# Even-step probabilities turned by VectorE and DMA instead of TensorE, and one outer loop written out

## The chip, the cores and the metric

The kernel runs on one core of a Trainium2 chip. The metric is the device time of one execution in microseconds (us); lower is better. A core has TensorE (matrix products and 128x128 transposes, written to PSUM), VectorE, ScalarE and GpSimd (elementwise work; in the profile DVE, ACT and POOL), SyncE (SP, which here only issues DMAs), an on-chip memory SBUF of 128 partitions, and the eight banks of PSUM. The engines run their own queues and wait for each other by semaphores.

## The reference

The input is `x` (32 x 64 tokens of width 512) with a context of the same shape. The reference computes

- `h = layernorm(x)`, `q = h Wq` in 32 heads of 128, `k = ctx Wk` and `v = ctx Wv` in 8 heads of 128 (each shared by 4 query heads);
- root-mean-square normalisation of `q` and `k` over the 128 elements of a head, with weights;
- `probs = softmax(q k / sqrt(128) + mask)` over the 64 keys of the same batch entry, `attn = probs v`, and `x = x + tanh(g_x) * attn Wo`;
- then a second layernorm and a feed-forward part: a shared SiLU network and 16 experts, of which each token takes its best two, added with `tanh(g_f)`.

Everything is float32. The change touches only the attention.

## The kernel before, in words

**Stages.** First the keys and values of all tokens are computed (to about 205 us), then come the attention steps (to about 1070 us), then the feed-forward part.

**Attention steps.** There are `STEPS` = 64 steps, i = 0 to 63: 8 groups of query heads (one for each key head) times 8 chunks of 256 tokens. The program counts them as i = 2 d + odd. In step i TensorE computes the queries of step i + 1 (`q_head`, twice, L610 to L612, each product as three products of a high and a low part), the product of step i - 1's probabilities with the values (`probs_v`, L738), the scores of step i + 1 (`scores`, L691), in even steps the transposes of step i's probabilities (`transpose_probs`, L723; in odd steps these stand between the two halves of the second `q_head`), and the output projection of step i - 1 (`outputs`, with `project_out` and `add_quarters`, L705, between its parts).

VectorE computes in step i: the sums of squares of the new queries (`turn_squares` L1526, a transpose of 32x32 blocks; `sum_squares` L1532; `split_sums` L1540 and L1542, whose result `sqs_hl` feeds `add_quarters`), the low part of the attention output (`a_rest`, L1517), the low part of the turned probabilities (`probs_lo`, L1596 in even and L1593 in odd steps), the sums of the squares per head (L1555, L1560), the addition of a projected tile to `acc` (`add_out`, L1511), and the softmax of step i + 1 (L1567 to L1587, result `pb`), at the end a slice of the next group's weights (`slice_lo`, L1601). GpSimd takes the inverse root between (L501) and splits the values (L507, L509). ScalarE copies and squares the queries (L1148, L1156), copies the attention output (L1183) and the turned probabilities (`probs_hi`, L1175 even, L1172 odd), splits weights (`split_slice`, L1187) and takes the exponentials (`exps`, L1161).

**Keys and probabilities as they lie.** The keys are turned by 32x32 blocks on VectorE (`turn_keys`), stored to the DRAM tensor `kbuf`, and loaded by `load_k` (L337) with the blocks in their turned places. The probabilities are turned by TensorE into PSUM: bank 6 in even steps, banks 2 and 3 in odd ones. Bank 6 also receives `project_out(0, ...)`.

**Loads.** SyncE's queue runs `next_loads(d, odd)`: in odd steps four `kt` loads; then a slice of weights (`wraw`, L379), once the slice before has been split (`w_hi`, `w_lo`); then the values `vt` (L385), once the values before have been split (`v_split`).

**Loops.** On each engine steps 0 to 7 stand first, then a hardware loop `Fori(0, 3)` over `gg`, whose body is two groups of 8 steps (steps 8 to 23, 24 to 39, 40 to 55), then the last group. Within a group an inner hardware loop runs over pairs of steps. All order is by hand: the queues are the program text, and the waits are on counts.

Of the kernel before, what the change touches and what calls it, by code (L numbers as in the profile page):

```python
# [32 lines left out]
F32 = mybir.dt.float32  # L33
# [8 lines left out]
P = 128  # L42
# [7 lines left out]
NC = T // CT  # L50
CB = CT // S
STEPS = KVH * NC
TURNED = (3, STEPS - NC)
E, EI = 16, 128
# [12 lines left out]
def build(nc, x, ctxT, wk, wv, w_att, w_shd, mask, g_x, g_f, q_w, k_w, gate, w_gu, w_dn, out):  # L67
    kbuf = nc.dram_tensor("kbuf", [KVH, NC // 2, 4, P, P], F32, kind="Internal").ap()
    vbuf = nc.dram_tensor("vbuf", [STEPS, P, CT], F32, kind="Internal").ap()
    h2buf = nc.dram_tensor("h2buf", [T, D], F32, kind="Internal").ap()  # L70
    ybuf = nc.dram_tensor("ybuf", [2 * T + 2 * P, D], F32, kind="Internal").ap()

    k_ld = kbuf.rearrange("g r l (q j) (c i) -> (g r) c j (l q) i", q=4, c=4)
    k_st = kbuf.rearrange("g r l p n -> r l p g n")
    v_st = vbuf.rearrange("(g c) p (b t) -> c b p g t", g=KVH, b=2)
# [3 lines left out]
    with ExitStack() as ctx:  # L79
# [144 lines left out]
        oh1 = sb("oh1", [P, NT, E])  # L224
        oh2 = sb("oh2", [P, NT, E])
        sgt = [sb(f"sgt{q}", [P, D]) for q in range(1)]
        aft = [sb(f"aft{q}", [P, D]) for q in range(1)]
# [57 lines left out]

        mark = sem("mark")
        ctx_first = [sem("ctx_first0"), sem("ctx_first1")]

        block = ctx.enter_context(nc.Block())

        def turned(j):
# [19 lines left out]
        def _(sp):  # L311

            for s in (v_stored, k_stored, *h2_stored, wgu_last):
                sp.sem_inc(s, 16)
# [55 lines left out]

            def next_loads(d, odd, x_tiles=()):

                i = 2 * d + odd
                if odd:
                    sp.wait_ge(s_done, i + 1)
                    load_k(d + 1)
                sp.wait_ge(w_hi, i + 8)
                sp.wait_ge(w_lo, i + 8)
                sp.dma_start(wraw[:], w_att[i + NC]).then_inc(wr_in, 16)  # L379
                for n in x_tiles:  # L380
                    if n >= 2:
                        sp.wait_ge(x1_done, n - 1)
                    sp.dma_start(xt3[n % 2][:], x[n]).then_inc(x3_in[n % 2], 16)
                sp.wait_ge(v_split, 2 * i + 2)
                sp.dma_start(vt[:].rearrange("p b t -> p (b t)"), vbuf[i + 1]).then_inc(vt_in, 16)  # L385

            with sp.Fori(0, (STEPS - NC) // 2) as d:
                for odd in range(2):
                    next_loads(d, odd)

            for t in range(NC - 1):
# [223 lines left out]
        def _(pe):  # L615
# [141 lines left out]

            def outputs(r, w_before, w_o, o_ready=None, turn=True):
                pe.wait_ge(acc_done, 2 * r + 1)
                project_out(1, w_before, (0, 1))  # L760
                if turn:
                    add_quarters(r + 2)
                project_out(1, w_before, (2, 3))
                if o_ready is not None:
                    pe.wait_ge(w_lo, o_ready)
                pe.wait_ge(pT_evac, 2 * r + 4)
                pe.wait_ge(a_hi, 4 * r + 6)
                pe.wait_ge(a_lo, 4 * r + 6)
                pe.wait_ge(acc_done, 2 * r + 2)
                project_out(0, w_o, (0, 1, 2, 3))  # L770

            def step(d, odd, pair_q, w_q, w_before, w_o, q_ready=None, o_ready=None, last=False, turn=True):


                i = 2 * d + odd
                if q_ready is not None:
                    pe.wait_ge(w_lo, q_ready)
                pe.wait_ge(q_sq, 2 * i + 1)
                q_head(0, 1 - odd, pair_q, w_q).then_inc(q_done, 1)
                pe.wait_ge(q_sq, 2 * i + 2)  # L780
                q_head(1, 1 - odd, pair_q, w_q, (0, 1))
                if last:
                    pe.wait_ge(ss_turned, i + 1)
                    transpose_h2(0, 2)
                    pe.wait_ge(s_scaled, i + 1)
                    transpose_h2(1, 3)
                if odd:
                    transpose_probs(i, odd)
                q_head(1, 1 - odd, pair_q, w_q, (2, 3)).then_inc(q_done, 1)
                probs_v(i - 1, 1 - odd)  # L790
                if last:
                    pe.wait_ge(h2T_lo, 2)
                scores(d + odd, 1 - odd)
                if not turn:
                    q_sums(i + 1)
                if last:
                    transpose_h2(2, 0)
                    transpose_h2(3, 1)
                if not odd:
                    pe.wait_ge(acc_done, 2 * i)  # L800
                    transpose_probs(i, odd)
                outputs(i - 1, w_before, w_o, o_ready, turn)

# [58 lines left out]
            group(0, 0, first=True)  # L862
            with pe.Fori(0, KVH // 2 - 1) as gg:
                for p in range(2):
# [214 lines left out]
        def _(act):  # L1079
# [87 lines left out]

            def probs_hi(i, odd, bank=2):
                act.wait_ge(pT_done, i + 1)
                if odd:  # L1170
# [19 lines left out]
            def act_step(d, odd, w, sl):  # L1190
# [4 lines left out]
                if odd:  # L1195
                    probs_hi(i, 1)
                q_out(1, i + 1)
                squares(1, i + 1)
                a_hi_tile(i - 1, 0)
                if not odd:  # L1200
                    probs_hi(i, 0)
                a_hi_tile(i - 1, 1)
                split_slice(i, w, sl)
                exps(i + 1)

# [35 lines left out]
            act_group(0, 0, 2)  # L1241
            with act.Fori(0, KVH // 2 - 1) as gg:
                for p in range(2):
# [140 lines left out]
        def _(dve):  # L1384
# [158 lines left out]

            def softmax(j, *meanwhile):
                per_row = lambda t: t[:].unsqueeze(2).to_broadcast([P, 8, S])
# [17 lines left out]
                if meanwhile:  # L1563
                    meanwhile[0]()
                dve.wait_ge(q_rt, j + 1)
                dve.wait_ge(s_done, j + 1)
                dve.tensor_tensor(pb[:], PS[3][:].rearrange("p (b s) -> p b s", s=S), per_row(qr),  # L1567
                                  ALU.mult).then_inc(s_scaled, 1)
# [20 lines left out]
            def probs_lo(i, odd, bank=2):  # L1589
# [4 lines left out]
                else:  # L1594
                    dve.wait_ge(pT_hi, 2 * i + 2)
                    dve.tensor_tensor(pt_even(1), pT_even(), pt_even(0), ALU.subtract).then_inc(pT_evac, 2)  # L1596

# [15 lines left out]
            def dve_step(d, odd, w, sl, tile_before, tile, complete=(None, None), turn=True):  # L1613

                i = 2 * d + odd
                if turn:
                    turn_squares(i + 1, 0)
# [12 lines left out]
                if complete[1] is not None:  # L1630
                    residual(complete[1], 0)
                if turn and not odd:
                    probs_lo(i, 0)
# [9 lines left out]

                softmax(i + 1, while_root, while_exp)
                if odd or not turn:
# [32 lines left out]
            dve.memset(g_hl[:].rearrange("p k e -> p (k e)").bitcast(F32), 0.0).then_inc(const_dve, 1)  # L1678
            with dve.Fori(0, KVH // 2 - 1) as gg:
                for p in range(2):  # L1680
# [349 lines left out]
```

## Time and profile before

| | us |
|---|---|
| median of 3 runs | 1386.31 (1386.3 to 1386.43) |
| the profiled execution, its own time | 1385.93 |
| its span | 1384.2 |
| TensorE busy | 1370.0 (99% of the span) |
| VectorE busy | 1020.1 (74%) |
| ScalarE busy | 506.7 (37%) |
| GpSimd busy | 359.3 (26%) |
| mean DMA rate over the span | 90 GB/s |

The span is the stretch from the first to the last recorded instruction of the profiled execution; its own time is what the device took with what lies around the span. Busy time of TensorE counts pipelined matmuls whose ends are modelled, so distances between the starts of neighbouring instructions say more than durations. TensorE's granted clock is 1.0 of full speed throughout.

### The profile page before, as it was taken

The page shows a single profiled execution, that of the slowest core. Times are in us where ns is not written, and L with a number is a line of the kernel's source. Part 1 is how long each engine was busy: PE and PEld are TensorE (multiplying, and loading weights), DVE is VectorE, ACT ScalarE, POOL GpSimd, SP SyncE. Part 2 cuts the span into 40 slices and gives each one's busy share as a digit, 9 for nine tenths or more (in the row PEclk, how much of TensorE's full clock was granted, in tenths as well). Part 3 has the DMA queues.
Part 4 walks back from the last instruction along what each step waited for, and adds up shares of the span by engine and source line. Part 5 has one row for each costly group of instructions (what it writes and reads, how often), then busy time and mean ns, then how long its engine had stood idle before and what let it go on. Part 6 is the DMA issues. An engine that isn't in the chain of part 4 may idle for free.

```text
span 1384.2 us, 26710 instructions
## 1 busy us (share of the span) xinstructions
PE 1370.0 (99%) x8629; PEld 1107.8 (80%) x8630; DVE 1020.1 (74%) x2151; ACT 506.7 (37%) x1085; POOL 359.3 (26%) x374
## 2 busy tenths in 40 slices
PE   9999999999999999999999999999999999999998
PEld 7888877888888887888887888888787888777777
DVE  7555558888888888888888888888688745244459
ACT  5323244343434343434343434434334421222242
POOL 1222232212121212121212121221212100467646
PEclk9999999999999999999999999999999999999999
DMA  6644431111111111111111111111223244554548
GB/s 223 206 135 148 132 94 39 44 38 44 31 43 39 42 38 37 39 42 39 35 44 39 40 33 46 36 42 31 65 62 100 99 160 188 174 193 167 167 147 309
DMA packets 150119, 125.54 MB, mean 91 GB/s; under 512 B 74256, under 2 KB 116240, under 8 KB 149776
## 3 DMA queue, kind: packets, MB, share of 16 engines
q1 hardware_dynamic: 142512, 99.71, 24.2%
q0 software_dynamic: 7520, 24.65, 5.3%
q8 instruction: 58, 0.95, 0.3%
q14 instruction: 29, 0.24, 0.1%
HBM read 86.84 MB, written 37.49 MB: 90 GB/s over the span
## 4 chain that ended last, share of the span: by engine, by line
PE 79%; DVE 4%; issue 1%; DMA 1%; ACT 0%; DVEq 0%; POOL 0%; ACTq 0%
PE ps L610 19%; PE ps L612 18%; PE ps L611 18%; PE ps L999 6%; PE ps L691 5%; PE ps L738 4%; PE ps L1015 3%; PE ps L723 2%; PE ps L994 1%; DVE acc L1960 1%; DVE acc L1967 1%; PE ps L912 1%; PE ps L746 0%; PE ps L1046 0%; PE ps L699 0%
## 5 line engine op out<-in xcount | busy, mean ns | idle before, releaser
L507 POOL CAST vth<-vt 128x256 fp32r<-128x256 f32 x64 | 25.4, 397 | 535.9 <-PE ps L738 533.9
L610 PE MATMUL ps<-hT,w0h 128*128 128x512 f32 (+1 forms) x384 | 152.2, 396 | 1.2 <-DVE w0l L1435 1.2
L1183 ACT CAST ah<-ps 128x256 fp32r<-128x256 f32 x256 | 83.0, 380 | 187.1 <-PE ps L612 180.7
L612 PE MATMUL ps<-hT,w0h 128*128 128x512 f32 (+1 forms) x384 | 149.9, 390 | 0.0
L611 PE MATMUL ps<-hT,w0l 128*128 128x512 f32 (+1 forms) x384 | 149.6, 390 | 0.0
L501 POOL TENSOR_TENSOR qr<-qv,mhalf 128x8 f32<-128x8 f32 x64 | 105.1, 1642 | 157.7 <-DVE qv L1560 131.0
L1148 ACT ACTIVATE qs<-ps,wqk 128x512 f32<-128x512 f32 x128 | 88.2, 689 | 119.3 <-PE ps L612 119.3
L1511 DVE TENSOR_TENSOR acc<-ps,acc 128x512 f32 (+1 forms) x128 | 88.0, 687 | 52.9 <-PE ps L612 52.5
L1161 ACT ACTIVATE pb<-pb 128x256 f32<-128x256 f32 x128 | 48.3, 418 | 167.2 <-DVE pb L1578 167.2
L610 PE MATMUL ps<-w0l,ah 128*128 128x512 f32 x256 | 105.7, 413 | 0.0
L610 PE MATMUL ps<-w1l,ah 128*128 128x512 f32 x256 | 105.0, 410 | 0.0
L1517 DVE TENSOR_TENSOR al<-ps,ah 128x256 fp32r<-128x256 f32 x256 | 96.0, 417 | 11.3 <-ACT ah L1183 10.3
L1526 DVE STREAM_TRANSPOSE sqT<-sq 128x512 f32<-128x512 f32 x108 | 76.6, 709 | 35.6 <-ACT sq L1156 31.4
L610 PE MATMUL ps<-hT,w1h 128*128 128x512 f32 (+1 forms) x256 | 101.3, 396 | 0.0
L612 PE MATMUL ps<-w0h,ah 128*128 128x512 f32 x256 | 100.2, 391 | 0.0
L612 PE MATMUL ps<-w1h,ah 128*128 128x512 f32 x256 | 100.1, 391 | 0.0
L611 PE MATMUL ps<-w0h,al 128*128 128x512 f32 x256 | 100.0, 391 | 0.0
L612 PE MATMUL ps<-hT,w1h 128*128 128x512 f32 (+1 forms) x256 | 100.0, 391 | 0.0
L611 PE MATMUL ps<-w1h,al 128*128 128x512 f32 x256 | 100.0, 391 | 0.0
L611 PE MATMUL ps<-hT,w1l 128*128 128x512 f32 (+1 forms) x256 | 99.7, 390 | 0.0
L999 PE MATMUL ps<-wgu,xgT 128*128 x376 | 94.9, 382 | 0.4 <-issue 0.4
L610 PEld LDWEIGHTS ps<-hT,w0h 128*128 128x128 f32 x384 | 72.1, 188 | 16.5 <-DVE w0l L1435 1.4
(248 smaller groups left out, 3183.7 us busy)
## 6 DMA issues: line engine op xcount, KB each, us to landing
wraw<-in_w_att SPq DMA_DIRECT2D x64, 256.0 KB, 2.6
vbuf<-vo SPq DMA_DIRECT2D x16, 512.0 KB, 3.3
kbuf<-ko SPq DMA_DIRECT2D x16, 512.0 KB, 5.1
kt<-kbuf SPq DMA_DIRECT2D x128, 64.0 KB, 2.2
vt<-vbuf SPq DMA_DIRECT2D x64, 128.0 KB, 2.1
wgu<-in_w_gu SPq DMA_DIRECT2D x4, 2048.0 KB, 8.5
y<-ybuf SPq DMA_DIRECT2D x16, 512.0 KB, 5.9
xt<-in_x SPq DMA_DIRECT2D x16, 256.0 KB, 5.3
```

The lines of the kernel that those rows point to most:

```text
L501: pool.tensor_tensor(qr[:], qv[:], mhalf[:, 0:8], ALU.pow).then_inc(q_rt, 1)
L610: pe.matmul(dst, l_hi, r_lo, start=first, stop=False)
L611: pe.matmul(dst, l_lo, r_hi, start=False, stop=False)
L612: return pe.matmul(dst, l_hi, r_hi, start=False, stop=last)
L691: mm = pe.matmul(PS[3][h * S:(h + 1) * S, b * S:(b + 1) * S], qs[:, h, b], kt[:, b, :], start=True, stop=True)
L738: mm = pe.matmul(PS[4 + b2][:, bp * 256:(bp + 1) * 256], vhl[v_part][rows, bp, :], pt[p_part][rows, 2 * part + bp, :], start=(z == 0), sto ...
L999: mm = pe.matmul(PS[2 + q][:, 0:2 * EI], xgT[q][:, k, :], wgu[:, bass.ds(e, 1), k * 2 * EI:(k + 1) * 2 * EI].rearrange("p a n -> p (a n)") ...
L1148: act.activation(qs[:, h].rearrange("p b s -> p (b s)"), PS[h][:], ACT.Copy, scale=wqk[:, 0:1]).then_inc(q_copy, 1)
L1183: act.copy(ah[:, bp, :, b2, :], pv_view(bp, b2)).then_inc(a_hi, 1)
L1511: dve.tensor_tensor(dst, PS[6 + bp][:], dst, ALU.add).then_inc(acc_done, 1)
L1517: dve.tensor_tensor(al[:, bp, :, b2, :], pv_view(bp, b2), ah[:, bp, :, b2, :], ALU.subtract).then_inc(a_lo, 1)
L1526: dve.transpose(sqT[:].rearrange("p n i -> p (n i)"), sq[:, h].rearrange("p b s -> p (b s)")).then_inc(sq_turned, 1)
```

## The change

In the even steps from 4 to 54 (`by_dma`, 26 steps) the probabilities `pb` are no longer turned by TensorE. VectorE turns them by 32x32 blocks into `pbT`, SyncE stores `pbT` to a DRAM tensor `pbuf` (256 KB), waits for the store to land, and loads the blocks back with four DMAs (64 KB each) into `pt_raw`, so that the whole is the 128x128 transposes' result. ScalarE's high copy and VectorE's low part read `pt_raw` instead of PSUM; `probs_hi` moves from between the two `a_hi_tile` to behind `split_slice` and ahead of `exps`, and `probs_lo` from behind `a_rest` to behind the softmax. On SyncE the store stands ahead of the `wraw` load of the even step, the wait for it and the four loads ahead of the `vt` load. TensorE no longer waits in those steps for bank 6 to be read before `project_out(0, ...)`. The odd steps, steps 0 and 2, and those of the last group are turned as before.

The loop over `gg` becomes a Python loop on TensorE, ScalarE and VectorE: its body stands three times in their programs. The inner loops stay, and so does GpSimd's; SyncE's loop over pairs is as before but begins at step 4.

```diff
--- before.py
+++ after.py
@@ -50,6 +50,7 @@
 NC = T // CT
 CB = CT // S
 STEPS = KVH * NC
+BY_DMA = (4, STEPS - NC)
 TURNED = (3, STEPS - NC)
 E, EI = 16, 128
 SI = 512
@@ -66,11 +67,13 @@
 
 def build(nc, x, ctxT, wk, wv, w_att, w_shd, mask, g_x, g_f, q_w, k_w, gate, w_gu, w_dn, out):
     kbuf = nc.dram_tensor("kbuf", [KVH, NC // 2, 4, P, P], F32, kind="Internal").ap()
+    pbuf = nc.dram_tensor("pbuf", [P, 4, P], F32, kind="Internal").ap()
     vbuf = nc.dram_tensor("vbuf", [STEPS, P, CT], F32, kind="Internal").ap()
     h2buf = nc.dram_tensor("h2buf", [T, D], F32, kind="Internal").ap()
     ybuf = nc.dram_tensor("ybuf", [2 * T + 2 * P, D], F32, kind="Internal").ap()
 
     k_ld = kbuf.rearrange("g r l (q j) (c i) -> (g r) c j (l q) i", q=4, c=4)
+    p_ld = pbuf.rearrange("(q j) c n -> c j q n", q=4)
     k_st = kbuf.rearrange("g r l p n -> r l p g n")
     v_st = vbuf.rearrange("(g c) p (b t) -> c b p g t", g=KVH, b=2)
     h2_t = h2buf.rearrange("(n p) d -> n p d", p=P)
@@ -223,6 +226,9 @@
         rb = sb("rb", [P, NT, E])
         oh1 = sb("oh1", [P, NT, E])
         oh2 = sb("oh2", [P, NT, E])
+        with ExitStack() as a:
+            pbT = sb("pbT", [P, 4, 4, 32], F32, a)
+            pt_raw = sb("pt_raw", [P, 4, 4, 32], F32, a)
         sgt = [sb(f"sgt{q}", [P, D]) for q in range(1)]
         aft = [sb(f"aft{q}", [P, D]) for q in range(1)]
         rab = sb("rab", [P, NT, E], BF16)
@@ -284,9 +290,22 @@
 
 
         mark = sem("mark")
+        p_turned, p_out, p_back = sem("p_turned"), sem("p_out"), sem("p_back")
         ctx_first = [sem("ctx_first0"), sem("ctx_first1")]
 
         block = ctx.enter_context(nc.Block())
+
+        def by_dma(i, odd):
+
+            return not odd and (not isinstance(i, int) or BY_DMA[0] <= i < BY_DMA[1])
+
+        def pT_before(i, d):
+
+            if not isinstance(i, int):
+                return d + 2
+            if BY_DMA[0] <= i < BY_DMA[1]:
+                return i // 2 + 2
+            return i if i < BY_DMA[0] else i - (BY_DMA[1] - BY_DMA[0]) // 2
 
         def turned(j):
 
@@ -310,7 +329,7 @@
         @block.sync
         def _(sp):
 
-            for s in (v_stored, k_stored, *h2_stored, wgu_last):
+            for s in (v_stored, k_stored, p_out, *h2_stored, wgu_last):
                 sp.sem_inc(s, 16)
 
             def first_context(tt):
@@ -368,12 +387,21 @@
             sp.wait_ge(hT_lo, NT)
             sp.dma_start(graw[:], gate).then_inc(g_in, 16)
 
-            def next_loads(d, odd, x_tiles=()):
+            def next_loads(d, odd, x_tiles=(), k=None):
 
                 i = 2 * d + odd
+                if k is not None:
+                    sp.wait_ge(p_turned, k + 1)
+                    sp.wait_ge(p_back, 64 * k + 64)
+                    sp.dma_start(pbuf, pbT[:].rearrange("p c m i -> p c (m i)")).then_inc(p_out, 16)
                 if odd:
                     sp.wait_ge(s_done, i + 1)
                     load_k(d + 1)
+                if False:
+                    if k is not None:
+                        probs_back(k)
+                    sp.wait_ge(v_split, 2 * i + 2)
+                    sp.dma_start(vt[:].rearrange("p b t -> p (b t)"), vbuf[i + 1]).then_inc(vt_in, 16)
                 sp.wait_ge(w_hi, i + 8)
                 sp.wait_ge(w_lo, i + 8)
                 sp.dma_start(wraw[:], w_att[i + NC]).then_inc(wr_in, 16)
@@ -381,12 +409,27 @@
                     if n >= 2:
                         sp.wait_ge(x1_done, n - 1)
                     sp.dma_start(xt3[n % 2][:], x[n]).then_inc(x3_in[n % 2], 16)
-                sp.wait_ge(v_split, 2 * i + 2)
-                sp.dma_start(vt[:].rearrange("p b t -> p (b t)"), vbuf[i + 1]).then_inc(vt_in, 16)
-
-            with sp.Fori(0, (STEPS - NC) // 2) as d:
+                if not False:
+                    if k is not None:
+                        probs_back(k)
+                    sp.wait_ge(v_split, 2 * i + 2)
+                    sp.dma_start(vt[:].rearrange("p b t -> p (b t)"), vbuf[i + 1]).then_inc(vt_in, 16)
+
+            def probs_back(k):
+                sp.wait_ge(p_out, 16 * k + 32)
+                sp.wait_ge(pT_evac, 4 * k + 6)
+                for c in range(4):
+                    sp.dma_start(pt_raw[32 * c:32 * c + 32].rearrange("p q m i -> p q (m i)"),
+                                 p_ld[c]).then_inc(p_back, 16)
+
+            sp.sem_inc(p_back, 64)
+            for d in range(BY_DMA[0] // 2):
                 for odd in range(2):
                     next_loads(d, odd)
+            with sp.Fori(0, (BY_DMA[1] - BY_DMA[0]) // 2) as k:
+                next_loads(k + BY_DMA[0] // 2, 0, k=k)
+                next_loads(k + BY_DMA[0] // 2, 1)
+            sp.wait_ge(pT_evac, 2 * BY_DMA[1] - 2)
 
             for t in range(NC - 1):
                 next_loads((STEPS - NC) // 2 + t // 2, t % 2, {0: (), 1: (0, 1), 2: ()}.get(t, (2 * t - 4, 2 * t - 3)))
@@ -755,7 +798,7 @@
                 if ks[-1] == KD - 1:
                     mm.then_inc(gu_done, 1)
 
-            def outputs(r, w_before, w_o, o_ready=None, turn=True):
+            def outputs(r, w_before, w_o, o_ready=None, turn=True, bank_free=False):
                 pe.wait_ge(acc_done, 2 * r + 1)
                 project_out(1, w_before, (0, 1))
                 if turn:
@@ -763,7 +806,8 @@
                 project_out(1, w_before, (2, 3))
                 if o_ready is not None:
                     pe.wait_ge(w_lo, o_ready)
-                pe.wait_ge(pT_evac, 2 * r + 4)
+                if not bank_free:
+                    pe.wait_ge(pT_evac, 2 * r + 4)
                 pe.wait_ge(a_hi, 4 * r + 6)
                 pe.wait_ge(a_lo, 4 * r + 6)
                 pe.wait_ge(acc_done, 2 * r + 2)
@@ -796,10 +840,11 @@
                 if last:
                     transpose_h2(2, 0)
                     transpose_h2(3, 1)
-                if not odd:
+                dma = turn and by_dma(i, odd)
+                if not odd and not dma:
                     pe.wait_ge(acc_done, 2 * i)
                     transpose_probs(i, odd)
-                outputs(i - 1, w_before, w_o, o_ready, turn)
+                outputs(i - 1, w_before, w_o, o_ready, turn, dma)
 
             for k in range(KD):
                 pe.wait_ge(w_lo, k + 1)
@@ -860,7 +905,7 @@
                     step(d0 + NC // 2 - 1, 1, 0, W[1 - p], W[p], W[p], q_ready=i0 + 12)
 
             group(0, 0, first=True)
-            with pe.Fori(0, KVH // 2 - 1) as gg:
+            for gg in range(KVH // 2 - 1):
                 for p in range(2):
                     group(NC // 2 + NC * gg + NC // 2 * p, 1 - p)
             group((STEPS - NC) // 2, 1, last=True)
@@ -1165,8 +1210,13 @@
                 q_out(h, 0)
                 squares(h, 0)
 
-            def probs_hi(i, odd, bank=2):
-                act.wait_ge(pT_done, i + 1)
+            def probs_hi(i, odd, bank=2, d=None):
+                if by_dma(i, odd):
+                    act.wait_ge(p_back, 64 * d)
+                    act.wait_ge(pv_done, 2 * i + 2)
+                    act.copy(pt_even(0).rearrange("p m (q i) -> p q m i", q=4), pt_raw[:]).then_inc(pT_hi, 2)
+                    return
+                act.wait_ge(pT_done, pT_before(i, d) + 1)
                 if odd:
                     for q in range(2):
                         act.copy(pt_odd(0, q), pT_odd(q, bank)).then_inc(pT_hi, 1)
@@ -1193,14 +1243,18 @@
                 q_out(0, i + 1)
                 squares(0, i + 1)
                 if odd:
-                    probs_hi(i, 1)
+                    probs_hi(i, 1, d=d)
                 q_out(1, i + 1)
                 squares(1, i + 1)
                 a_hi_tile(i - 1, 0)
-                if not odd:
+                if not odd and not by_dma(i, odd):
                     probs_hi(i, 0)
                 a_hi_tile(i - 1, 1)
+                if by_dma(i, odd) and False:
+                    probs_hi(i, 0, d=d)
                 split_slice(i, w, sl)
+                if by_dma(i, odd):
+                    probs_hi(i, 0, d=d)
                 exps(i + 1)
 
             def act_group(d0, p, t0=0):
@@ -1239,7 +1293,7 @@
             exps(3)
             act_step(1, 1, W[1], 3)
             act_group(0, 0, 2)
-            with act.Fori(0, KVH // 2 - 1) as gg:
+            for gg in range(KVH // 2 - 1):
                 for p in range(2):
                     act_group(NC // 2 + NC * gg + NC // 2 * p, 1 - p)
 
@@ -1541,7 +1595,7 @@
                 dve.wait_ge(sq_sums, k + 3)
                 dve.tensor_tensor(sqs_hl[:, 1, :], flat, sqs_hl[:, 0, :], ALU.subtract).then_inc(sq_part, 1)
 
-            def softmax(j, *meanwhile):
+            def softmax(j, *meanwhile, turn_before=None):
                 per_row = lambda t: t[:].unsqueeze(2).to_broadcast([P, 8, S])
                 dve.wait_ge(ss_done, j + 2)
 
@@ -1564,6 +1618,8 @@
                     meanwhile[0]()
                 dve.wait_ge(q_rt, j + 1)
                 dve.wait_ge(s_done, j + 1)
+                if turn_before is not None:
+                    dve.wait_ge(p_turned, turn_before)
                 dve.tensor_tensor(pb[:], PS[3][:].rearrange("p (b s) -> p b s", s=S), per_row(qr),
                                   ALU.mult).then_inc(s_scaled, 1)
                 if len(meanwhile) > 2:
@@ -1593,6 +1649,11 @@
                         dve.tensor_tensor(pt_odd(1, q), pT_odd(q, bank), pt_odd(0, q), ALU.subtract).then_inc(pT_evac, 1)
                 else:
                     dve.wait_ge(pT_hi, 2 * i + 2)
+                    if by_dma(i, odd):
+                        dve.tensor_tensor(pt_even(1).rearrange("p m (q i) -> p q m i", q=4), pt_raw[:],
+                                          pt_even(0).rearrange("p m (q i) -> p q m i", q=4),
+                                          ALU.subtract).then_inc(pT_evac, 2)
+                        return
                     dve.tensor_tensor(pt_even(1), pT_even(), pt_even(0), ALU.subtract).then_inc(pT_evac, 2)
 
             def slice_lo(i, w, sl):
@@ -1613,6 +1674,11 @@
             def dve_step(d, odd, w, sl, tile_before, tile, complete=(None, None), turn=True):
 
                 i = 2 * d + odd
+                if by_dma(i, odd):
+                    dve.wait_ge(p_ready, 2 * i + 2)
+                    dve.wait_ge(p_out, 16 * (d - 1))
+                    dve.transpose(pbT[:].rearrange("p c m i -> p (c m i)"),
+                                  pb[:].rearrange("p (m z) (h j) -> p (z h) m j", z=2, h=2)).then_inc(p_turned, 1)
                 if turn:
                     turn_squares(i + 1, 0)
                 if odd:
@@ -1629,7 +1695,7 @@
                 a_rest(i - 1, 0)
                 if complete[1] is not None:
                     residual(complete[1], 0)
-                if turn and not odd:
+                if turn and not odd and not by_dma(i, odd):
                     probs_lo(i, 0)
 
                 def while_root():
@@ -1641,7 +1707,9 @@
                 def while_exp():
                     add_out(2 * i, 0, tile)
 
-                softmax(i + 1, while_root, while_exp)
+                softmax(i + 1, while_root, while_exp, turn_before=d - 1 if by_dma(i, odd) else None)
+                if by_dma(i, odd):
+                    probs_lo(i, 0)
                 if odd or not turn:
                     slice_lo(i, w, sl)
 
@@ -1676,7 +1744,7 @@
             dve.wait_ge(pool_const, 6)
             dve.tensor_copy(trib[:], tri[:]).then_inc(const_dve, 1)
             dve.memset(g_hl[:].rearrange("p k e -> p (k e)").bitcast(F32), 0.0).then_inc(const_dve, 1)
-            with dve.Fori(0, KVH // 2 - 1) as gg:
+            for gg in range(KVH // 2 - 1):
                 for p in range(2):
                     group(NC // 2 + NC * gg + NC // 2 * p, 1 - p)
             dve.wait_ge(g_hi_ok, 1)
```

## Rows read from the trace of the kernel before

**Rows 1.** The page: busy us, share of the span and instructions of each engine.
```profile
PE 1370.0 (99%) x8629; PEld 1107.8 (80%) x8630; DVE 1020.1 (74%) x2151; ACT 506.7 (37%) x1085; POOL 359.3 (26%) x374
```

**Rows 2.** Attention: us, busy PE, PEld, DVE, ACT, POOL, clock, DMA share, GB/s.
```profile
240.00:1070.00 830.00, 828.11 (x5890) 675.24 (x5889) 699.33 (x1521) 329.63 (x759) 167.40 (x181) 1.00 0.17 44
```

**Rows 3.** Waits of TensorE: us in total, times, the longest.
```profile
PE ps L705 <- DVE sqs_hl L1542: 1.4, 2, 0.9
```

**Rows 4.** Timeline, TensorE, an odd step: start us, us, engine, instruction.
```profile
600.18 1.15 PE L691 MATMUL ps<-kt,qs 128*64 128x64 f32 x32
...
601.27 0.50 PE L610 MATMUL ps<-w1l,ah 128*128 128x512 f32 x1
```

**Rows 5.** Timeline, TensorE, the even step behind it.
```profile
613.46 1.15 PE L691 MATMUL ps<-kt,qs 128*64 128x64 f32 x32
...
614.96 0.47 PE L610 MATMUL ps<-w1l,ah 128*128 128x512 f32 x1
...
616.19 0.19 PEld L705 LDWEIGHTS ps<-sqs_hl,fold 128*128 128x128 f32 x1
```

**Rows 6.** Timeline, VectorE, around the start of the same even step.
```profile
610.95 0.69 DVE L1601 TENSOR_TENSOR w0l<-wraw,w0h 128x512 f32 x1
611.55 0.71 DVE L1526 STREAM_TRANSPOSE sqT<-sq 128x512 f32<-128x512 f32 x1
...
613.85 0.71 DVE L1526 STREAM_TRANSPOSE sqT<-sq 128x512 f32<-128x512 f32 x1 [0.86 <-ACT sq L1156]
...
615.53 0.19 DVE L1542 TENSOR_TENSOR sqs_hl<-sqs,sqs_hl 128x32 fp32r<-128x32 f32 x1
...
616.33 0.68 DVE L1596 TENSOR_TENSOR ptl<-ps,pth 128x512 fp32r<-128x512 f32 x1
616.93 0.27 DVE L1555 SCALAR_TENSOR_TENSOR ssg<-ps,quarters 128x64 f32<-128x64 f32 x1
```

**Rows 7.** Timeline, all engines, from there into the odd step.
```profile
618.26 0.69 DVE L1511 TENSOR_TENSOR acc<-ps,acc 128x512 f32 x1 [0.80 <-PE ps L612]
...
618.78 0.64 ACT L1187 CAST w0h<-wraw 128x512 f32 x1
...
622.15 0.75 ACT L1161 ACTIVATE pb<-pb 128x256 f32<-128x256 f32 x2 [2.73 <-DVE pb L1578]
...
624.72 0.60 PE L723 MATMUL ps<-ident,pb 128*128 128x128 f32 x4
...
625.76 0.76 DVE L1593 TENSOR_TENSOR ptl<-ps,pth 128x256 fp32r<-128x256 f32 x2 [0.29 <-ACT pth L1172]
...
627.96 0.71 DVE L1526 STREAM_TRANSPOSE sqT<-sq 128x512 f32<-128x512 f32 x1 [0.25 <-ACT sq L1156]
```

**Rows 8.** SyncE's timeline, and DMA issues (KB each, us to landing).
```profile
611.85 0.33 SPq L379 DMA_DIRECT2D wraw<-in_w_att  x1
...
615.68 1.92 SPq L337 DMA_DIRECT2D kt<-kbuf  x4
...
kbuf<-ko SPq DMA_DIRECT2D x16, 512.0 KB, 5.1
kt<-kbuf SPq DMA_DIRECT2D x128, 64.0 KB, 2.2
...
h2buf<-h SPq DMA_DIRECT2D x12, 256.0 KB, 2.6
```

**Rows 9.** Busy time by stretch: sixteen steps each, scores to scores.
```profile
310.88:530.05 219.17, 219.17 (x1554) 179.43 (x1553) 186.25 (x407) 86.77 (x201) 44.18 (x48) 1.00 0.16 40
530.05:750.59 220.54, 219.64 (x1555) 179.30 (x1553) 187.47 (x408) 86.79 (x201) 44.18 (x48) 1.00 0.16 40
750.59:970.49 219.90, 219.36 (x1555) 179.40 (x1553) 187.68 (x409) 86.94 (x202) 44.18 (x48) 1.00 0.16 39
```

**Rows 10.** Timeline, VectorE, in an inner loop and at the outer loop's third round.
```profile
354.91 0.76 DVE L1517 TENSOR_TENSOR al<-ps,ah 128x256 fp32r<-128x256 f32 x2 [0.26 <-issue]
...
750.75 0.71 DVE L1526 STREAM_TRANSPOSE sqT<-sq 128x512 f32<-128x512 f32 x1 [2.23 <-issue]
```

## The prediction

> **What bounds the kernel now.** I read the page's busy line first: TensorE is busy for 1370.0 of 1384.2 us, VectorE for 74% [rows 1]. The stretches by stage say where the change lands: from 240 to 1070 us, the attention steps, TensorE is busy for 828.11 of 830 us and VectorE for 699.33 [rows 2]. The waits of TensorE are short; the only one inside this stretch is on VectorE's `sqs_hl`, 1.4 us in two waits [rows 3]. So TensorE's own queue sets the end, and a step shortens by what leaves that queue, until another engine's result comes later than TensorE asks for it. The rest of the work is to price what leaves, and to find that other engine's margins.
>
> **TensorE: what leaves the queue.** The edit takes the four transposes of `transpose_probs` out of 26 even steps (i = 4, 6, ... 54). I don't price them by their durations, since matmuls overlap, but by the distance between neighbours. In an odd step, where no transposes follow the scores, the scores start at 600.18 and the next product (L610) at 601.27: 1.09 us [rows 4]. In an even step they start at 613.46 and L610 at 614.96: 1.50 us, with the four transposes between [rows 5]. The transposes cost 0.41 us a step, 0.10 each. 26 x 0.41 = 10.7 us.
>
> The Trainium skill, "VectorE: DVE Perf Modes", section "Rules for kernel authors", advises TensorE for a 128x128 transpose whose result may go to PSUM, which speaks against this change. "TensorE: Matmul & The Clock Gate" (Part 4) gives about 275 ns for one in a kernel; as an estimate from that page, 104 of them would be worth 28.6 us. The spacing of the rows, 0.10 us each, disagrees with that as a price in the queue, and I go by the rows.
>
> **VectorE: what is added and moved.** Added per even step: one transpose of `pb`, 128x512 f32. The nearest row is L1526, the same operation and size without the reordered input: 0.71 us, and 0.74 to the instruction that needs it [rows 6]. Lower bound 0.71, since the elements are the same; the upper bound is twice that, 1.42, if the reordered reads ran at half speed, which no row shows. I take 0.71. Moved: `probs_lo` (0.60 us of the queue, from the start before it to L1555) goes from behind `a_rest` to behind the softmax. Its source becomes SBUF; L1601 has SBUF sources and the same size, 0.69 us, so I change nothing for that.
>
> The new transpose stands behind L1601 and ahead of the first L1526. L1526 at 611.55 moves to 612.29; its reduction (L1532) follows 0.74 later and takes 0.69, so it ends at 613.72. The second L1526 waits for ScalarE's square and starts at 613.85, after 0.86 us of idle time [rows 6]: the added 0.74 lies in that idle time, with 0.1 us to spare. So L1542 still ends at 615.72. TensorE's `add_quarters` (weight load at 616.19, [rows 5]) needs it, and would now come 0.41 earlier, at 615.78. Margin: 0.06 us, and a wake-up costs about as much. A stall of 0 to 0.1 us is possible here; I take 0.02, or 0.5 us over 26 steps.
>
> Then the softmax of the odd step. Its first instruction behind the root is fixed by `add_out` (L1511), which waits for TensorE (idle 0.80 us) and so comes 0.41 earlier with it; the rest of the softmax follows in VectorE's own order [rows 7]. The root on GpSimd must be there by then. It runs 0.6 us earlier, since `probs_lo` no longer stands ahead of L1555. The whole chain to the probabilities thus moves with TensorE, which asks for them at 624.72, now 624.31 [rows 7]. Behind the softmax, `probs_lo` delays the next L1526 by 0.43 us against TensorE; two later waits on ScalarE (0.29 us at L1593, 0.25 us at the second L1526 of the odd step) take most of it. TensorE needs `ptl` only at `probs_v`, 1.9 us after it is ready.
>
> **ScalarE and the trip through memory.** The copy `probs_hi` (L1175) keeps its 0.59 us but stands behind `split_slice` (L1187, 618.78 plus 0.64) and ahead of `exps`. Shifted by 0.41, ScalarE is free at 619.0; `exps` starts at 622.15, now 621.74, so the copy must start by 621.1 [rows 7]. If it is later, the exponentials queue behind it, then the softmax, then TensorE's odd transposes.
>
> The trip: the transpose on VectorE runs 611.55 to 612.26. SyncE wakes after 0.2 (L1601 ends at 611.64, the `wraw` load follows at 611.85 [rows 8]). A store of 256 KB lands in 2.6 us (`h2buf`): 615.1. Wake-up 0.2; four loads at 0.48 each (the `kt` row: 1.92 for four), the last issued at 616.7; it lands 2.2 us later (`kt`), at 618.9 to 619.0 [rows 8]. That is the time at which ScalarE gets there, 2.1 us ahead of the limit. Upper bound of the store: `kbuf<-ko`, 5.1 us for 512 KB in 512-byte pieces, which puts the end at 621.5, 0.4 past the limit. I take 2.6, as 256 KB in 2 KB rows is nearest to `h2buf`.
>
> Behind the new waits on SyncE stand, in even steps, `wraw` (behind `p_turned`: 611.85 moves to about 612.8, lands 2.6 us later, needed at 618.4), and behind the landing and the four issues `vt`, which GpSimd splits one step later, and the four `kt` loads (615.68 moves to 617.6, and TensorE needs them for the scores at about 627). All are hidden; if the store took 5.1 us they would still be. The DMA share in this stretch is 0.17 [rows 2], so 512 KB more per 27.4 us find room.
>
> **The loop written out.** The outer loop's second and third rounds begin at steps 24 and 40. At the latter VectorE stands idle for 2.23 us ahead of its first L1526, at 750.75, with no releaser but the issue itself [rows 10]: a jump back. Sixteen steps, from scores to scores, take 219.17 us in the first round, 220.54 and 219.90 in the other two [rows 9]. Against the first: 1.37 + 0.73 = 2.1 us, which the straight code removes. ScalarE's and TensorE's own jumps are within the same numbers. Bounds: 0, if a straight program pays for its code elsewhere, and 2.1.
>
> **The sum.** -10.7 + 0.5 - 2.1 = -12.3. The profiled execution took 1385.93 us (span 1384.2, 1.7 around it), 0.4 below the median of the runs; against itself that gives 1373.6, against the median 1386.31 - 12.3 = 1374.0. I forecast 1374.0, own range 1371.5 to 1376.5. The rest of the program only moves forward.
>
> **Rivals.**
> A: VectorE's margin goes. It holds only 0.1 us ahead of the second L1526 and 0.06 at `add_quarters`. A transpose of over 0.9 us, from the reordered input, reaches TensorE with each further tenth; at 1.42 it costs 0.55 a step, more than the 0.41 saved, and the kernel takes 1388. For it: the margins. Against: the same count of elements, and the odd step lives with the same margin already. Halfway it gives 26 x 0.2 = 5 us back: 1376.5 to 1383.5. Chance 0.17.
> B, the other side: the trip is late. From 2.1 us of lateness on, each further us holds `exps` and TensorE in each of 26 steps; at 2.5 us the 0.41 of a step is gone; at 2.7 us, 26 x 0.6 = 15.6 us are lost and the kernel takes 1389.6; at the upper bound of the store (0.4 past the limit) it takes 1384. For it: two trips in a row, each of which has to land before the next may start. Against: medians of 2.6 and 2.2 and an idle queue. Chance 0.10 for slower.
> C: the straight code costs. VectorE's six inner loops now lie at other places in the code; one whose jump back reaches code no longer held would pay 2.3 us of VectorE, about 2 us of TensorE with the margins gone, at two jumps a loop: 4 us a loop, 1377 to 1383 for one or two. Against it: of the jumps of the inner loops in the trace none shows idle time on VectorE, only 0.26 us once a round, at 354.91 [rows 10]. The Trainium skill, "Runtime: NRT & Kernel Launch", section "Instruction fetch mechanics", says that a taken branch to code outside the fetched window waits for it, and that straight code is fetched ahead. The 2.23 us of the row agree with that. Chance 0.12.
> D: nothing gained, because TensorE then waits for something I don't see: 1383.5 to 1389. Chance 0.06.
> The forecast keeps 0.55.
>
> **The numbers.** 0.2% of this kernel is 2.8 us, about what a measurement can tell from no change: faster below 1383.5, slower above 1389.1. Faster: 0.55, nearly all of A and C, 0.84 together; same 0.06; slower 0.10. The range reaches over A and C to 1382 and down to 1371, where stalls that I left standing would also be gone; it leaves out B, D and the ends of A and C.
>
> **What would show it.** After the change L610 should follow the scores by 1.09 us in even steps too, and sixteen steps should take 219.17 - 8 x 0.41 = 215.9 us in each of the three rounds; what is above that is a new wait. L705 with idle time released by `sqs_hl` is A; L1161 late behind L1175, with a DMA as releaser, is B; idle time on VectorE without a releaser at an inner loop's start is C. At steps 24 and 40 VectorE should show no 2.2 us. What would make me wrong above all is the duration of the reordered transpose, or a landing over 4.5 us.

## The result and the profile after

The changed kernel takes 1373.13 us (median of 4 runs, 1372.46 to 1376.79), the one before 1386.30 on the same chip (4 runs). The ratio is 0.9907, with a 95% interval of 0.9889 to 0.9925: 13.2 us faster, where 12.3 were forecast. The profiled execution took 1373.33 us, its span 1371.6.

The page's busy line of the changed kernel answers to [rows 1].

```profile
PE 1358.2 (99%) x8525; PEld 1098.0 (80%) x8526; DVE 1030.1 (75%) x2177; ACT 505.7 (37%) x1085; POOL 360.4 (26%) x374
```

TensorE has 104 matmuls fewer and VectorE 26 instructions more, and TensorE is still the bound. The time is seen best in the rounds of sixteen steps, scores to scores, which answer to [rows 9]:

```profile
310.81:526.74 215.93, 215.93 (x1522) 176.26 (x1520) 190.98 (x418) 86.30 (x201) 44.21 (x48) 1.00 0.23 60
526.74:742.42 215.68, 215.68 (x1523) 176.33 (x1521) 190.46 (x417) 86.43 (x201) 44.22 (x48) 1.00 0.23 59
...
sum 647.27, PE 647.27 PEld 528.91 DVE 570.25 ACT 259.23 POOL 132.64; mean PE 215.76 PEld 176.30 DVE 190.08 ACT 86.41 POOL 44.21
```

The second column of times is TensorE's busy time: it equals the length of every stretch (the third round is 215.66 us long), where two rounds of before had gaps. The three rounds shrank from 659.61 to 647.27 us together. 215.9 us a round was the forecast. The rounds hold 24 of the 26 changed steps; steps 4 and 6, ahead of them, are shorter by 0.41 and 0.40 us (distance of their scores to the next), which together with the 12.3 us of the rounds makes the 13.2.

An even step of the changed kernel on TensorE, which answers to [rows 5]:

```profile
607.64 1.15 PE L734 MATMUL ps<-kt,qs 128*64 128x64 f32 x32
608.72 0.50 PE L653 MATMUL ps<-w1l,ah 128*128 128x512 f32 x1
...
610.21 0.19 PE L748 MATMUL ps<-sqs_hl,fold 128*128 128x64 f32 x1
```

From the scores to the next product it is 1.08 us now, 1.50 before. `add_quarters` (L748 here) shows no idle time ahead of it in this step; `sqs_hl` was written at 609.93, and its weight load starts at 609.98. In one of the 26 steps it did wait, the one from scores 9 to scores 10:

```profile
309.18 0.48 DVE L1746 MEMSET g_hl<- 128x512 f32 x1
313.51 0.19 PEld L748 LDWEIGHTS ps<-sqs_hl,fold 128*128 128x128 f32 x1 [0.40 <-DVE sqs_hl L1596]
```

There VectorE does two small instructions more (a copy at 308.91 and the memset shown), which take 0.68 us of its queue ahead of the new transpose. The step is 0.25 us longer than in a kernel without the new work. The kernel before had the same two instructions there, and no such wait. An ordinary even step on VectorE, for [rows 6]:

```profile
605.75 0.70 DVE L1680 STREAM_TRANSPOSE pbT<-pb 128x512 f32<-128x512 f32 x1
606.38 0.67 DVE L1580 STREAM_TRANSPOSE sqT<-sq 128x512 f32<-128x512 f32 x1
...
608.05 0.71 DVE L1580 STREAM_TRANSPOSE sqT<-sq 128x512 f32<-128x512 f32 x1 [0.28 <-ACT sq L1201]
...
609.74 0.19 DVE L1596 TENSOR_TENSOR sqs_hl<-sqs,sqs_hl 128x32 fp32r<-128x32 f32 x1
```

The new transpose (L1680) takes 0.70 us, as the one with plain input does, and the next one starts 0.63 behind it. The idle time ahead of the second L1580 went from 0.86 to 0.28 us: the new work sits in a gap. ScalarE's copy of the loaded blocks, behind `split_slice`, and the exponentials, for [rows 7]:

```profile
613.10 0.63 ACT L1217 CAST pth<-pt_raw 128x512 fp32r<-128x512 f32 x1
615.94 0.76 ACT L1206 ACTIVATE pb<-pb 128x256 f32<-128x256 f32 x2 [2.21 <-DVE pb L1634]
```

The DMA issues of both legs of the trip, KB each and us from issue to landing:

```profile
pbuf<-pbT SPq DMA_DIRECT2D x26, 256.0 KB, 2.0
pt_raw<-pbuf SPq DMA_DIRECT2D x104, 64.0 KB, 2.0
```

ScalarE's copy of the loaded blocks (L1217) has no idle time ahead of it, so the blocks were there when it came, and the exponentials still wait 2.21 us for VectorE. The start of the former third round on VectorE, for [rows 10]:

```profile
740.52 0.70 DVE L1680 STREAM_TRANSPOSE pbT<-pb 128x512 f32<-128x512 f32 x1
```

Where 2.23 us without a releaser stood there is nothing.

### The profile page after: what moved, and what is told of

It reads as the page before. It is cut to its first block, busy times and chain, and to the rows that moved or that the text cites. A ratio compares the mean times of both kernels' runs of the same rounds, so it can differ in the third digit from the quotient of the medians.

```text
span 1371.6 us, 26399 instructions
## 1 busy us (share of the span) xinstructions
PE 1358.2 (99%) x8525; PEld 1098.0 (80%) x8526; DVE 1030.1 (75%) x2177; ACT 505.7 (37%) x1085; POOL 360.4 (26%) x374
## 4 chain that ended last, share of the span: by engine, by line
PE 80%; DVE 2%; issue 1%; DMA 1%; ACT 0%; POOL 0%; DVEq 0%; ACTq 0%
PE ps L653 20%; PE ps L655 19%; PE ps L654 19%; PE ps L1044 6%; PE ps L734 5%; PE ps L781 4%; PE ps L1060 3%; PE ps L1039 1%; PE ps L766 1%; DVE acc L2028 1%; DVE acc L2035 1%; PE ps L957 1%; PE ps L789 0%; PE ps L1091 0%; PE ps L742 0%
## 5 line engine op out<-in xcount | busy, mean ns | idle before, releaser
L1580 DVE STREAM_TRANSPOSE sqT<-sq 128x512 f32<-128x512 f32 x108 | 75.5, 699 | 15.2 <-ACT sq L1201 15.1
```

The costliest lines, as they stand in the source:

```text
L1580: dve.transpose(sqT[:].rearrange("p n i -> p (n i)"), sq[:, h].rearrange("p b s -> p (b s)")).then_inc(sq_turned, 1)
```

## The experiments

Two kernels leave work out, and so don't compute the reference's output; they are named. The kernel before was timed anew beside each group of them, with medians from 1385.99 to 1386.66 us, so parts of a microsecond are read from the rounds. "Rounds" below is the length of the three stretches of sixteen steps together: 659.61 us before, 647.27 changed. It leaves out the first stage, whose length varied by 2 us from run to run.

### One edit at a time

**Only the loops.** The kernel before with

```diff
-            with pe.Fori(0, KVH // 2 - 1) as gg:
+            for gg in range(KVH // 2 - 1):
```

and the same on ScalarE and VectorE.

> The kernel before with the loop over gg written out on TensorE, ScalarE and VectorE, and nothing else. My theory: 2.1 us of the gain come from this alone, so about 1384.2 us, with no 2.2 us of idle time on VectorE at steps 24 and 40. Rival: the gain of the outer loop exists only beside the other edit, or it is the run's noise: 1386.3 us.

It took 1384.16 us (before, here 1386.66; ratio 0.998, 0.997 to 0.999), and its rounds are all alike:

```profile
312.70:531.57 218.87, 218.87 (x1554) 179.40 (x1553) 187.32 (x409) 86.76 (x201) 44.22 (x48) 1.00 0.16 39
...
750.46:969.30 218.84, 218.84 (x1555) 179.41 (x1553) 185.87 (x407) 86.91 (x202) 44.22 (x48) 1.00 0.17 39
```

The sum of the three is 656.60, 3.0 us under before. VectorE shows no 2.2 us of idle time any more. The gain is there without the other edit. It is more than the 2.1 that I read from [rows 9], because even the first round of before (219.17) carried 0.3 us of loop.

**Only the turned probabilities.** The changed kernel with the three loops as hardware loops again (the diff above backwards).

> The changed kernel with its three outer loops as hardware loops again. My theory: 10.7 us of the gain come from the 26 steps without TensorE's transposes; VectorE's margins are smaller now, so its jump back of 2.2 us costs TensorE more than before, 1.5 to 2 us each time instead of about 1: 1376 to 1377.5 us. Rival: the two edits simply add up, 1375.6 us or less.

1378.68 us, ratio 0.9943 (0.9927 to 0.996), and rounds of 651.94. Its steps are as short as those of the changed kernel, except at the two jumps. VectorE's timeline at the second, and then TensorE's waits:

```profile
744.61 0.71 DVE L1680 STREAM_TRANSPOSE pbT<-pb 128x512 f32<-128x512 f32 x1 [2.21 <-issue]
```

```profile
PE ps L748 <- DVE sqs_hl L1596: 3.5, 2, 1.8
```

VectorE still loses 2.2 us at a jump, and TensorE now waits 1.8 us for it, where it waited at most 0.9 before [rows 3]. Against the changed kernel the loops are worth 651.94 - 647.27 = 4.7 us of the rounds, against 3.0 without the other edit. The two edits don't simply add up. Part of the difference comes without any new work on VectorE: between the two kernels below that only leave TensorE's transposes out, the loops are worth 650.40 - 646.84 = 3.6 us, with waits of 1.1 us at most. So of the 1.7 us more, about 0.6 go with the shorter step on TensorE and 1.1 with the transpose on VectorE, which uses the slack that had softened the jump. The kernel was slower than the 1377.5 us that I had expected at most: a jump cost TensorE 2.1 and 2.0 us, not 1.5 to 2.

**Which engine's loop.** The kernel before with VectorE's loop alone written out:

> The kernel before with the loop over gg written out on VectorE alone; TensorE and ScalarE keep theirs. My theory: VectorE's jump is the costly one, so 1384.2 to 1384.6 us. Rival: TensorE's or ScalarE's own jump holds TensorE just as long, and 1385.5 to 1386.3 us come out.

1385.25 us (0.9989, 0.9979 to 0.9998), between the two ranges that I had given, and rounds 658.40: only 1.2 of the 3.0 us. By the rounds, my theory that VectorE's jump is nearly all of it falls. Steps 24 and 40 are still 0.33 and 0.45 us too long in the distance of their scores. The other way round, the changed kernel with TensorE's loop kept as a hardware loop:

> The changed kernel with the loop over gg a hardware loop again on TensorE alone. In the run with VectorE alone written out, steps 24 and 40 stayed 0.33 and 0.45 us longer. My theory: that is TensorE's own jump, and this kernel is 0.8 to 1.5 us slower than the changed one, 1374 to 1374.6 us. Rival: it was ScalarE's jump, and this kernel equals the changed one.

1375.69 us, rounds 648.78, 1.5 us over the changed kernel: 0.36 and 0.44 at the two jumps, the rest in hundredths over all steps. That is more than I had expected (1374.6 at most), but in the direction of my theory. So TensorE's own loop is worth 1.5 us in the changed kernel; its queue shows no idle time for it, only wider distances. (With VectorE's loop alone written out it shows 0.17 us, at the second jump.) Why the loop widens the steps between the jumps too stays open. ScalarE's loop was not kept alone; with TensorE's it is worth 658.40 - 656.60 = 1.8 us in the kernel before, so little seems left for it.

### What the replacement costs

**No transposes, and nothing in their place.** The kernel before with, in the 26 steps,

```diff
-                    transpose_probs(i, odd)
+                    pe.wait_ge(p_ready, 2 * i + 2)
+                    pe.sem_inc(pT_done, 1)
```

so that their probabilities are left out.

> The kernel before without TensorE's four transposes in the 26 even steps from 4 to 54, and with nothing in their place: ScalarE and VectorE read what lies in PSUM bank 6, so the probabilities of these steps are left out. My theory: the transposes cost TensorE 0.41 us a step and the replacement costs nothing, so 1386.3 - 10.7 = 1375.6 us, the same distance from the changed kernel as the loops are worth (2 us). Rival: the replacement on VectorE and the DMA queues does cost something that the 0.41 hides, and this kernel is well below 1375.

1377.18 us (0.9926, 0.991 to 0.9943), rounds 650.40. Away from the jumps its steps are those of the changed kernel: 13.25 and 13.72 us. The 1.6 us over the 1375.6 that I had expected are the jumps, dearer here than the 2 us that I had put in for them (3.6, above). With the loops written out as well, again without those probabilities:

> The kernel before with the three loops over gg written out and without TensorE's transposes in the 26 even steps, nothing in their place (the probabilities of these steps are left out). It is what the changed kernel would be if its VectorE transpose and its DMAs were free. My theory: equal to the changed kernel within 1 us, about 1373 us, since all of the replacement is hidden. Rival: the changed kernel pays for it somewhere, and this one is 2 us or more below it.

1373.58 us (0.9907, 0.989 to 0.9924), and beside it on the same chip the changed kernel:

> The changed kernel once more, for the comparison on one chip: 1372.5 to 1374 us. The start of the first scores varied from 198.1 to 200.2 us between the profiled runs so far, whatever the kernel, so differences under 1 us say little.

1373.51 us (0.9911, 0.9895 to 0.9928). The rounds are 646.84 and 647.42. All of the new work, 26 transposes on VectorE and 130 DMAs, costs 0.4 to 0.6 us of the rounds (two profiles of the changed kernel), 0.25 of it in one step (from scores 9 to scores 10, 13.94 us long, with the wait shown above), and nothing that the timed runs can tell. Against the loops alone, the missing transposes give 656.60 - 646.84 = 9.76 us for the 24 even steps in the rounds, 0.41 each.

### How near the limits were

**VectorE.** The new transpose done twice:

```diff
+                                  pb[:].rearrange("p (m z) (h j) -> p (z h) m j", z=2, h=2)).then_inc(p_first, 1)
+                    dve.wait_ge(p_first, d - 1)
+                    dve.transpose(pbT[:].rearrange("p c m i -> p (c m i)"),
```

> The changed kernel with VectorE's new transpose done twice in a row in each of the 26 steps. In the changed kernel's trace 0.28 us of idle time are left ahead of VectorE's second transpose of the squares and about 0.05 at TensorE's add_quarters. My theory: 0.74 us more on VectorE therefore cost TensorE 0.74 - 0.33 = 0.4 us a step, 26 x 0.4 = 10.7 us: all of the gain from TensorE is lost and about 1384 us come out, with waits of add_quarters on sqs_hl. Rival: VectorE is only 84% busy here and catches up in later idle time: within 2 us of 1373.

1383.79 us (0.9979, 0.9969 to 0.9988): 10.7 us lost, the number expected. The rounds are 657.27, which is 10.0 / 24 = 0.42 us a step. The wait stands where it should, at `add_quarters` (L749 here). In all, the waits of its weight loads:

```profile
PEld ps L749 <- DVE sqs_hl L1597: 15.6, 27, 1.2
```

So rival A was a real one: 0.7 us more on VectorE and the gain on TensorE is gone, although VectorE is busy for only 88% of the changed kernel's rounds.

**The trip.** One and then two more DMAs of 256 KB with a wait, behind the landing of the store:

```diff
+                for lag in range(1):
+                    sp.dma_start(pbuf2, pbuf).then_inc(p_lag, 16)
+                    sp.wait_ge(p_lag, 16 * k + 16 * lag + 16)
```

> The changed kernel with one more trip in each of the 26 steps: behind the landing of the store, SyncE copies pbuf to another DRAM tensor and waits for that before it loads the blocks back, some 2.5 us later. In the changed kernel's trace the last load lands 3.2 us ahead of the limit that the exponentials set. My theory: the 2.5 us are hidden, 1373 to 1374 us. Rival: ScalarE's copy, which then waits, or the loads behind it, already hold TensorE: above 1380.

1377.17 us (0.993, 0.9914 to 0.9947), 4 us lost. Neither side is quite right. In 20 of the 26 steps the delay is hidden from TensorE. One of them:

```profile
615.96 0.62 ACT L1222 CAST pth<-pt_raw 128x512 fp32r<-128x512 f32 x1 [1.83 <-DMA pt_raw<-pbuf]
...
616.87 0.75 ACT L1211 ACTIVATE pb<-pb 128x256 f32<-128x256 f32 x2 [0.29 <-DVE pb L1639]
```

ScalarE waits 1.83 us for the blocks, and the exponentials still have 0.29 us left. So it is in 12 of the 26 steps, with 0.2 to 0.6 us left; in the other 14 the exponentials follow the copy without idle time in the trace. The trips vary: the longest wait for the blocks is 3.4 us. Six steps are longer than in the changed kernel, by 0.3 to 1.0 us, 3.8 together, and they are the whole loss; in three of them, at 349, 674 and 945 us TensorE's transposes of the odd step waited for the softmax, 0.5 to 0.6 us at a time. With two more:

> The same with two more trips, some 5 us later. My theory: 1.8 us past the limit, less 0.1 to 0.2 us of margin at TensorE's odd transposes; 26 x 1.6 = 42 us more, 1410 to 1425 us, and ScalarE's copy of pt_raw waits for a DMA. Rival: the exponentials are not what hangs on the trip, and less than 10 us are lost.

1468.64 us (1.0598, 1.058 to 1.0616). The order of things is as expected, the size is not: 95.5 / 26 = 3.7 us a step, not 1.6. One copy from DRAM to DRAM landed in 2.9 us, not 2.5, which with the wake-ups puts the blocks 2.6 us or more past the limit instead of 1.8. TensorE's transposes of the odd steps wait 55.3 us in all for the softmax, 2.1 a step. The rest of the 95.5, some 40 us, is for the most part TensorE's clock. Two stretches behind such a wait, in different steps, the last columns granted clock, DMA share and GB/s, and then TensorE's timeline at the second:

```profile
333.00:337.00 4.00, 4.00 (x53) 3.21 (x52) 3.81 (x8) 2.32 (x6) 1.13 (x2) 1.00 0.07 12
668.00:672.48 4.48, 4.48 (x23) 3.18 (x23) 3.35 (x8) 1.82 (x4) 0.00 (x0) 0.62 0.02 4
```

```profile
667.96 0.77 PE L771 MATMUL ps<-ident,pb 128*128 128x128 f32 x4 [2.03 <-DVE pb L1648]
...
668.84 0.63 PE L659 MATMUL ps<-hT,w0l 128*128 128x512 f32 x1
669.27 0.63 PE L660 MATMUL ps<-hT,w0h 128*128 128x512 f32 x1
```

TensorE stands idle for 2.03 us, and behind that the granted clock of the next 4.5 us is 0.62 in the mean, the lower of its two levels (1.2 GHz) for most of it: products follow each other at 0.43 us instead of 0.23. It did not fall behind every such idle time. In 21 of the 26 steps it fell, and there the step is longer than in the changed kernel by its idle time and 1.5 to 1.9 us more. In five it stayed at 1.00, the one at 333 us among them, with the longest idle time of all (3.06 us); there the step is longer by its idle time and 0.3 us. Rival B, had it come true, would have been dearer than I priced it.

No kernel tried here beats the changed one. The same treatment of the odd steps was not tried: there the product with the values follows the transposes within the same step, with half a `q_head` between (six products at 0.23 us), while the two landings of the trip alone take 4.0 us.

## Why the prediction was right

**TensorE's four transposes, 0.41 us a step.** Shown: 0.41 by the kernel that leaves them out, and 0.39 net in the changed one (656.60 - 647.27 over 24 steps). The spacing of neighbours in the queue was the right price.

**VectorE's new transpose at 0.71 us, hidden.** Shown: 0.70, in the idle time. The margin ahead of the second L1580 was larger than I worked out (0.28 us left instead of 0.1), mostly because two transposes in a row follow at 0.63, not at 0.74. The margin at `add_quarters` was as small as I had it, 0.05 us. The stall term of 0.5 us was too large and spread wrongly: 25 steps show no wait there, and the one in which VectorE has 0.68 us of other work lost 0.25. Rival A's price was too high as well: 0.55 us a step for a transpose of 1.42 us, 1388 in all, where the doubled transpose, 1.38 us more on VectorE's queue than before, cost 0.42 and took 1383.79. And the low part `ptl` is ready 1.4 us ahead of its use (619.07 and 620.43), not 1.9; it still does no harm.

**The trip, 2.1 us ahead of the limit.** The store landed in 2.0 us, not 2.6. One more trip, 3.0 us in the median of that run, left 0.29 us in the step shown, so the margin there is 3.2 to 3.3 us. In the 14 steps without such a rest the margin was smaller or the extra trip longer.

**The loops, 2.1 us.** The mechanism was right, the size was not: 3.0 us without the other edit. "Against the first" was the weak step, since the first round of before is not free of the loop. I had read the jump from VectorE's idle time and left TensorE's and ScalarE's without a price of their own; my expectation for the runs then put nearly all on VectorE, which the run with VectorE alone contradicts: TensorE's own loop is worth 1.5 us in the changed kernel. The forecast of 215.9 us a round was built on the same first round: with its 0.3 us of loop taken off it would have been 215.6, what the kernel without transposes and without their replacement shows (646.84 over three); the cost of the replacement and that 0.3 nearly cancel in it, which is luck. That the jumps would become dearer once VectorE's slack was used stood in rival C only, for inner loops; the measured 4.7 us shows that it holds for the outer one, though only about 1.1 of it goes with VectorE's new work.

**Rival C** did not come: no idle time without a releaser is left on VectorE in the rounds, neither at the inner loops nor where the outer loop jumped. The Trainium skill ("Runtime: NRT & Kernel Launch", "Instruction fetch mechanics") has straight code fetched ahead. For the places where the outer loop jumped this trace agrees: no idle time stands at 740.52, where it was 2.23 us.

The forecast sum was 10.7 + 2.1 - 0.5 = 12.3; the parts measured one by one are 10.7 and 3.0, 13.7, and the two kernels' medians differ by 13.2. The 0.5 us between are what the replacement costs in the rounds (0.4 to 0.6), half of it in the one long step. Taken in the other order the parts are different, 659.61 - 651.94 = 7.7 us of the rounds for the turned probabilities and 4.7 for the loops; only their sum is a property of the change.

## What to carry to other kernels

Price what leaves a pipelined queue by the distance between its neighbours, not by durations: four transposes of 0.27 us each were worth 0.41 us together. When work moves to an engine that is not the bound, what counts is the idle time just ahead of the result that the bound waits for, not the busy share; double the moved work once, and the margin is measured. Look for the step in which that engine has something extra to do: the only wait of this change stood there. And look at a loop's jump on every engine before and after: what one engine's slack had hidden comes out when the slack is spent.

## What was unexpected of the hardware

With two more trips a step, TensorE's granted clock fell to the lower level for most of the 4.5 us behind an idle time of 2.03 us. In the same run it fell behind one of 1.73 us (at 514.0) and stayed at 1.00 behind one of 3.06 us (at 332.2), so the length of the idle time does not decide it; what does stays open. In the kernel with the turned probabilities and its hardware loops it stayed at 1.00 behind the two idle times of 1.8 and 1.7 us. And TensorE's hardware loop over a long body costs without any idle time in that run's records: 0.36 and 0.44 us at the two jumps.
